# One buffer for the absorbed queries, filled by halves, and queries and turned latents fetched from device memory

## The reference

```python
def xattn(ctx, latents, Wq, Wkv, Wo, ln1, ln2):        # 16 heads of 64
    xn, ln = layernorm(ctx, ln1), layernorm(latents, ln2)
    q = ln @ Wq
    k, v = split(concat([xn, ln], rows) @ Wkv)          # 1024 + 64 rows
    w = softmax(q @ k.T / 8)                            # per batch and head
    return (w @ v) @ Wo
x = x + xattn(ctx, layernorm(x), ...)
x = x + mamba(layernorm(x), ...)                        # 512 inner channels, 16 states
x = x + experts(layernorm(x), ...)                      # 8 experts, given lists
```

## Time and profile before

| | us |
|---|---|
| median of 3 runs | 893.54 (893.11 to 894.03) |
| the profiled execution: time, span | 892.84, 891.1 |
| TensorE busy, share of the span | 788.4, 88% |
| VectorE busy | 531.5, 60% |
| ScalarE busy | 398.1, 45% |
| GpSimd busy | 254.1, 29% |
| mean granted TensorE clock | 0.951 |

### The profile page before, as it was taken

How to read it: one execution, slowest core, us unless ns; L and a number is a source line. 1 busy time by engine, 2 the same in 40 slices (tenths; PEclk the granted TensorE clock), 3 DMA queues, 4 the chain that set the end, 5 groups by cost and what they waited for, 6 DMA issues and landing times.

```text
span 891.1 us, 13590 instructions
## 1 busy us (share of the span) xinstructions
PE 788.4 (88%) x5347; PEld 684.3 (77%) x5347; DVE 531.5 (60%) x992; ACT 398.1 (45%) x952; POOL 254.1 (29%) x173
## 2 busy tenths in 40 slices
PE   5889999999999999999999999997455667598996
PEld 3589999999999999999999999983122323267885
DVE  5365565565565565466556544428899999971112
ACT  3445545543544544454554444434834334403341
POOL 3718018018016105204404400001355555600000
PEclk9999999999999999999999999997759888888998
DMA  9100100100100000010030100000200000070720
GB/s 310 55 1 1 54 1 2 54 2 1 50 5 1 24 32 1 1 54 1 1 125 1 11 1 1 1 1 4 94 0 0 1 0 0 0 270 26 271 95 26
DMA packets 23779, 35.25 MB, mean 40 GB/s; under 512 B 6744, under 2 KB 19616, under 8 KB 22688
## 3 DMA queue, kind: packets, MB, share of 16 engines
q1 hardware_dynamic: 23712, 34.34, 11.7%
HBM read 32.77 MB, written 0.52 MB: 37 GB/s over the span
## 4 chain that ended last, share of the span: by engine, by line
PE 74%; DVE 19%; issue 4%; ACT 1%; DMA 1%; SPq 0%; DVEq 0%; POOL 0%; POOLq 0%
PE psum L1167 21%; PE psum L1201 19%; DVE state L793 11%; PE psum L1184 6%; PE psum L1140 3%; PE psum L1482 3%; PE psum L1472 3%; PE psum L1223 3%; PE psum L1378 2%; PE psum L1123 2%; PE psum L1147 2%; PE psum L1233 2%; PE psum L1214 1%; PE psum L1295 1%; DMA wq_sb<-in_L_xattn_Wq_dram 1%
## 5 line engine op out<-in xcount | busy, mean ns | idle before, releaser
L911 ACT ACTIVATE pt_hi<-psum 128x512 fp32r<-128x512 f32 (+1 forms) x192 | 87.3, 489 | 225.6 <-PE psum L1184 170.4
L1201 PE MATMUL psum<-kvn_hi,pt_hi 128*128 128x256 f32 x512 | 149.6, 292 | 0.0
L1201 PE MATMUL psum<-kvn_hi,pt_lo 128*128 128x256 f32 x512 | 144.1, 281 | 0.0
L1201 PE MATMUL psum<-kvn_lo,pt_hi 128*128 128x256 f32 x512 | 143.9, 281 | 0.0
L643 DVE TENSOR_REDUCE rowmax<-psum 128x1 f32<-128x728 f32 x64 | 58.7, 917 | 110.9 <-PE psum L1167 110.9
L793 DVE TENSOR_TENSOR_SCAN state<-dec,drive 128x2048 f32<-128x2048 f32 x16 | 107.1, 6693 | 0.1
L1201 PEld LDWEIGHTS psum<-kvn_lo,pt_hi 128*128 128x128 f32 x512 | 97.2, 190 | 0.1
L1201 PEld LDWEIGHTS psum<-kvn_hi,pt_hi 128*128 128x128 f32 x512 | 97.1, 190 | 0.1
L1201 PEld LDWEIGHTS psum<-kvn_hi,pt_lo 128*128 128x128 f32 x512 | 97.0, 189 | 0.0
L1167 PE MATMUL psum<-kvt_hi,qk_hi 128*128 128x364 f32 (+1 forms) x384 | 90.9, 345 | 4.5 <-ACT prob L951 2.7
L546 POOL TENSOR_TENSOR drive<-dtx,bmat 128x2048 f32<-128x2048 f32 x15 | 68.4, 4558 | 60.7 <-DVE state L793 60.7
(11 more groups left out here) (214 smaller groups left out, 1452.1 us busy)
## 6 DMA issues: line engine op xcount, KB each, us to landing
w<-in_L_ffn_W_dram SPq DMA_DIRECT2D x16, 1024.0 KB, 7.5
ctx_nat<-in_ctx_dram SPq DMA_DIRECT2D x8, 1024.0 KB, 5.4
wk_nat<-in_L_xattn_Wkv_dram SPq DMA_DIRECT2D x1, 1024.0 KB, 6.3
wq_sb<-in_L_xattn_Wq_dram SPq DMA_DIRECT2D x1, 1024.0 KB, 11.6
wv<-in_L_xattn_Wkv_dram SPq DMA_DIRECT2D x1, 1024.0 KB, 13.7
wo<-in_L_xattn_Wo_dram SPq DMA_DIRECT2D x1, 1024.0 KB, 16.1
lat_cur<-x_lat SPq DMA_DIRECT2D x16, 64.0 KB, 5.0
q_t<-in_L_attn_W_in_dram SPq DMA_DIRECT2D x1, 1024.0 KB, 6.9
```

Source lines behind the costliest of these rows:

```text
L911: act.activation(pt_hi[u][:, t0:t1, :], where[:, 0:(t1 - t0) * P].rearrange("p (t m) -> p t m", m=P), ACT.Copy)\
L1201: pe.matmul(PV, w[u][:, j, :], x_[slot][:, j, :], start=(j == 0 and w is pt_hi and x_ is kvn_hi), stop=False)
```

## The change

`qk_hi` and `qk_lo` have one slot instead of two, 16 KB of each partition less; a filler keeps what follows in place. The halves of a batch's absorbed queries are made at different times: pairs 0 to 3 (jobs 0, 2) for the next batch in steps 3 and 4, when the logits of these pairs are done, and pairs 4 to 7 (jobs 1, 3) in steps 0 and 1 of the batch itself, before its step 4. The order of jobs is `TURNS`, from step 2 of a batch to step 1 of the next: 4, 0, 2, 5, 6, 7, 1, 3. Batch 0 has no job in its steps 0 and 1, and batch 7 has two. Both statistics move into step 0, the first half ahead of the row maximum, and the scaling moves to step 1. `q_t` and `latt` are stored to device memory once; each batch's queries and own rows are loaded from there by SP, and the copies of GpSimd and ScalarE go. The store of `q_t` and the load of the next context are on the same queue, in this order.

```diff
+    TURNS = (4, 0, 2, 5, 6, 7, 1, 3)
+        q_keep = nc.dram_tensor("q_keep", [P, HP, T], F32, kind="Internal").ap()
+        latt_keep = nc.dram_tensor("latt_keep", [P, 2, CK, T], F32, kind="Internal").ap()
-        qk_hi = [sb(att, f"qk_hi{i}", [P, CK, HP, 2, L], F32R) for i in range(2)]
+        qk_hi = sb(att, "qk_hi", [P, CK, HP, 2, L], F32R)
...
         def misc_count(b, m):
-            return MISC * b + m + 1
+            return MISC * b + TURNS.index(m) + 1
+        def misc_of(b, hp, more):
+            if hp < 2:
+                return (b, TURNS[MISC - 2 + hp]) if 0 < b < B else None
+            return (b + 1, TURNS[hp - 2]) if more else None
...
@@ sync
+            def load_own(b):
+                for part, dst in enumerate((kvt_hi, kvt_lo)):
+                    sp.dma_start(dst[b % 2][:, :, S:].bitcast(F32), latt_keep[:, part, :, b * L:(b + 1) * L]).then_inc(ld_own, 16)
+            def load_queries(b):
+                for h in range(2):
+                    rows = slice(h * DH, (h + 1) * DH)
+                    sp.dma_start(q_cur[rows, :, h, :], q_keep[rows, :, b * L:(b + 1) * L]).then_inc(ld_q, 16)
             load_latents(0)
+            sp.wait_ge(s_pevac, 2)
+            sp.dma_start(latt_keep[:, 0], latt_hi[:].bitcast(F32)).then_inc(st_keep, 16)
+            sp.wait_ge(s_plo, 1)
+            sp.dma_start(latt_keep[:, 1], latt_lo[:].bitcast(F32)).then_inc(st_keep, 16)
+            sp.wait_ge(s_pqe, HP)
+            sp.dma_start(q_keep, q_t[:]).then_inc(st_keep, 16)
             for b in range(1, B):
-                sp.wait_ge(s_misc, MISC * b)
+                sp.wait_ge(s_misc, misc_count(b - 1, 7) if b > 1 else MISC)
                 sp.wait_ge(s_klo, b)
                 sp.dma_start(ctx_nat[:], ctx_in[b].rearrange("(p j) c -> p j c", j=SJ))\
                     .then_inc(ld_ctx, 16)
                 sp.wait_ge(s_lcur, 2 * b)
                 load_latents(b)
+                if b == 1:
+                    sp.wait_ge(st_keep, 48)
+                if b >= 2:
+                    sp.wait_ge(s_lg, HP * (b - 1))
+                load_own(b)
+                sp.wait_ge(s_misc, misc_count(b - 1, 3))
+                load_queries(b)
-            sp.wait_ge(s_qcur, 2 * B)
+            sp.wait_ge(s_misc, MISC * B)
@@ gpsimd: def queries(b), two copies into q_cur, and its call go
@@ vector, step
+                if more and hp == 0:
+                    ctx_stats(b + 1, 0)
                 if live:
                     dve.wait_ge(s_lg, count(b, hp))
...
-                if more and hp < MISC - 1:
-                    if hp < 2:
-                        ctx_stats(b + 1, hp)
-                    misc_lo(b + 1, 1 - slot, hp)
-                    if hp == 2:
-                        ctx_scale(b + 1)
+                if more and hp == 0:
+                    ctx_stats(b + 1, 1)
+                if job and hp < MISC - 1:
+                    misc_lo(job[0], job[0] % 2, job[1])
+                if more and hp == 1:
+                    ctx_scale(b + 1)
@@ scalar, step 7
-                    own_rows(b + 1, 1 - slot)
@@ tensor
                     if m == 0:
-                        pe.wait_ge(s_qcur, 2 * b + 2)
+                        if b == 0:
+                            pe.wait_ge(s_qcur, 2)
+                        else:
+                            pe.wait_ge(ld_q, 32 * b)
...
                     if hp == 0:
-                        pe.wait_ge(s_mlo, MISC * (b + 1))
-                        pe.wait_ge(s_own, 2 * (b + 1))
+                        pe.wait_ge(s_mlo, misc_count(b, 7) if b > 0 else MISC)
+                        if b == 0:
+                            pe.wait_ge(s_own, 2)
+                        else:
+                            pe.wait_ge(ld_own, 32 * b)
+                    if hp == HP // 2:
+                        pe.wait_ge(s_mlo, misc_count(b, 3))
```

More of the change, by code:

```diff
@@ L75, in perceiver_kernel @@
         kvt_lo = [sb(att, f"kvt_lo{i}", [P, CK, S + L], F32R) for i in range(2)]
-        qk_hi = [sb(att, f"qk_hi{i}", [P, CK, HP, 2, L], F32R) for i in range(2)]
-        qk_lo = [sb(att, f"qk_lo{i}", [P, CK, HP, 2, L], F32R) for i in range(2)]
+        qk_hi = sb(att, "qk_hi", [P, CK, HP, 2, L], F32R)
+        qk_lo = sb(att, "qk_lo", [P, CK, HP, 2, L], F32R)
         x_lat = sb(att, "x_lat", [P, TT, C])
@@ L83, in perceiver_kernel @@
         latt_lo = sb(att, "latt_lo", [P, CK, T], F32R)
+        sb(att, "rest_of_att", [P, 16 * C])
         q_cur = sb(att, "q_cur", [P, HP, 2, L])
@@ L251, in perceiver_kernel @@
         ld_lat = sem("ld_lat")
+        st_keep, ld_q, ld_own = sem("st_keep"), sem("ld_q"), sem("ld_own")
         ld_mam, ld_idx, ld_comb, ld_b2, ld_out = (sem(n) for n in ("ld_mam", "ld_idx", "ld_comb", "ld_b2", "ld_out"))
@@ L310, in misc_dst @@
                 k, a = m // 2, m % 2
-                return (qk_hi if hi else qk_lo)[slot][:, k, a * HP // 2:(a + 1) * HP // 2]\
+                return (qk_hi if hi else qk_lo)[:, k, a * HP // 2:(a + 1) * HP // 2]\
                     .rearrange("p h a l -> p (h a l)")
@@ L445, in _ @@
             pool.tensor_scalar(lshift[:], lnm[:], -1.0, 0.0, ALU.mult, ALU.add).then_inc(s_psc, 1)
[L447 to L456, removed]
             def latents(b, slot):
@@ L506, in body @@
                 if more:
-                    queries(b + 1)
                     context(b + 1, 1 - slot)
@@ L664, in step @@
                                       ALU.add).then_inc(s_woe, 1)
-                if more and hp == MISC - 1:
-                    misc_lo(b + 1, 1 - slot, hp)
+                job = misc_of(b, hp, more)
+                if job and hp == MISC - 1:
+                    misc_lo(job[0], job[0] % 2, job[1])
                 if p1:
                     tail_lo("C", p1)
-                if more and hp < MISC - 1:
-                    if hp < 2:
-                        ctx_stats(b + 1, hp)
-                    misc_lo(b + 1, 1 - slot, hp)
-                    if hp == 2:
-                        ctx_scale(b + 1)
+                if more and hp == 0:
+                    ctx_stats(b + 1, 1)
+                if job and hp < MISC - 1:
+                    misc_lo(job[0], job[0] % 2, job[1])
+                if more and hp == 1:
+                    ctx_scale(b + 1)
             def body(b, slot, more, pair):
@@ L953, in step @@
                 if more and hp == MISC - 1:
-                    misc_hi(b + 1, 1 - slot, hp)
-                    own_rows(b + 1, 1 - slot)
+                    misc_hi(b + 1, 1 - slot, TURNS[hp - 2])
                 if p1:
@@ L959, in step @@
                     keep_out(p3, pair if hp >= 3 else None)
-                if more and hp < MISC - 1:
-                    misc_hi(b + 1, 1 - slot, hp)
+                job = misc_of(b, hp, more)
+                if job and hp < MISC - 1:
+                    misc_hi(job[0], job[0] % 2, job[1])
             def body(b, slot, more, pair):
@@ L1130, in misc @@
                     pe.wait_ge(s_woe, after)
-                if not (isinstance(b, int) and b == 0):
+                if b > 0:
                     pe.wait_ge(s_mlo, misc_count(b, m) - 1)
@@ L1162, in logits @@
                     for q, x_ in ((qk_hi, kvt_hi), (qk_hi, kvt_lo), (qk_lo, kvt_hi)):
[L1163 removed]
+                        w = q[:, k, hp].rearrange("p a l -> p (a l)")
                         first, final = k == 0 and q is qk_hi and x_ is kvt_hi, k == CK - 1 and q is qk_lo
@@ L1251, in step @@
                     turn_value(p3)
+                job = misc_of(b, hp, more)
                 if slot == 0 and hp == 3 and pair is not None:
-                    out_proj(pair, misc_count(b + 1, hp) - 1)
-                if more and hp == MISC - 1:
-                    misc(b + 1, 1 - slot, hp)
+                    out_proj(pair, misc_count(*job) - 1)
+                if job and hp == MISC - 1:
+                    misc(job[0], job[0] % 2, job[1])
                 if p2:
@@ L1261, in step @@
                     head_out(p3)
-                if more and hp < MISC - 1:
-                    misc(b + 1, 1 - slot, hp, pair + 1 if slot == 0 and hp == 3 and pair is not None else None)
+                if job and hp < MISC - 1:
+                    misc(job[0], job[0] % 2, job[1], pair + 1 if slot == 0 and hp == 3 and pair is not None else None)
             def body(b, slot, more, pair):
```

## The result

The changed kernel takes 909.41 us (median of 4 runs, 907.21 to 911.79) against 893.78 us before (893.11 to 895.04): ratio 1.0174, interval 1.0138 to 1.0209. A second set of 4 runs of the same kernel gave 911.86 against 893.83, ratio 1.0206 (1.0191 to 1.0221). The eight runs are 907.21, 907.49, 910.48, 911.07, 911.33, 911.79, 912.64 and 913.62. Forecast were 907.4 in a range of 899 to 913. The profiled execution took 911.79 with a span of 910.1, 19.0 us more than before.

What follows compares the result with a forecast made beforehand. TensorE was taken to bound the attention part, so only its added waits or work cost time: 8.5 + 3.4 + 0.2 + 1.8 = 13.9 us on the median 893.54 gives 907.4, range 904 to 910 (899 to 913 with A and most of B).

Steps and rivals of the forecast that it cites:

- part 1: Step 2, batches 0 to 6: context transposes wait for GpSimd's add because scaling moves only one step earlier; 8.5 us slower.
- part 2: Batch 0: statistics ahead of the first row maximum wait for the context, plus query store; 3.4 us; later batches free.
- clock: Batch 0: one stretch of TensorE's lower clock after the longer wait, now wholly behind the restart; 0.2 us.
- part 3: Batch 7, steps 0 and 1: two query jobs gained at 0.89 us each, 1.8 us; batch 0's two lost save nothing.
- part 4: GpSimd's and ScalarE's copies become stores and loads on SP's queue; gain 0, cost 0, nothing waits for the loads.
- its own signs: Seven step-2 waits, context wait until 43 to 45 us, second logits near 49.4; wrong if start over 9 us late.
- A: Rival: the step-2 wait does not appear, something else holds TensorE or scaling comes earlier; 898.9 us, chance 0.09.
- B: Rival: the query store is slow and the start pays its upper bound, context 6.2 us later; 912.6 us, chance 0.10.
- D: Rival: ScalarE and VectorE's exchange sets step length, so removed copies and moved statistics save time; 893.4 or 891.6 us, chance 0.04.
- E: Rival: the step-2 wait is absent and the start hidden too, only part 3 is left; 895.3 us, chance 0.05.
- C: Rival: each of seven new waits brings a stretch of TensorE's lower clock, 12 us more; 919 us, chance 0.04.
- the fast bound of the prediction: Query store at 434 GB/s, gone by 38.3 before the context's bytes move, cost 0; the slow bound was 175 GB/s.

Runs made afterwards that it cites:

- e1: The changed kernel with the prologue's eight jobs counted 1 to 8 again in ScalarE's and VectorE's waits: 908.61 us against 893.96, ratio 1.0169.
- e3: The changed kernel with VectorE scaling the next context ahead of the job's low half in step 1: 904.53 us against 893.96, ratio 1.0122.
- e4: e1 with the store of the queries issued behind the load of context 1 and the latents: 909.07 us against 908.61 for e1.
- e5: The kernel before, with only the prologue waits of ScalarE and VectorE asking for counts in the new job order: 899.52 us against 893.96, ratio 1.0064.
- e6: Edits of e1, e2 and e3, and batch 0's jobs 1 and 3 moved from prologue to its steps 0 and 1: 893.99 us against 893.83, ratio 1.0001.
- e2: e1 with batch 0's first half of the statistics behind the first row maximum again: 904.55 us against 893.96, ratio 1.0125.

## Why the prediction was right, and where it was not

The time lay in the range, 2.0 us above the forecast by the first set and 4.5 by the second. That it lies so near is in part luck: a cost that was not forecast stands where a forecast one is hidden. The mechanism is borne out by e1, the kernel that the prediction had in mind: from its first logits to the end of the attention its steps fall behind by 13.8 us against the kernel before (14.2 from span to span, 14.7 by the medians), where 13.9 was forecast. Its parts one by one, with e1 where the changed kernel covers a part:

| step | forecast, us | measured, us |
|---|---|---|
| part 1, batches 1 to 6 | 7.74 | 7.69 (1.17 for odd, 1.38 for even ones) |
| part 1, batch 0 | 0.75 | 0.85 in e1 (steps 2 to 5) |
| part 2, batch 0, and clock | 3.4 + 0.2 | 3.48 in e1 (steps 0 and 1) |
| part 2, batches 1 to 7 | 0 | 0.00 |
| part 3 | 1.8 | 1.80 |
| part 4 | 0 | 0, no wait for the loads |
| prologue | 0 | 5.74, of which 4.9 by the counts |

**Part 1** was right in mechanism and size. GpSimd's add ends at 137.55 + 2.35 = 139.90, and the transpose that TensorE could have begun at 138.90 starts at 140.05. All engines of the changed kernel, batch 1, to be set against the earlier trace rows:

```profile
132.32 2.67 DVE L623 TENSOR_SCALAR ctx_nat<-ctx_nat,crstd,cshift 128x256 f32<-128x256 f32 x8
...
135.07 2.40 POOL L510 TENSOR_TENSOR ctx_nat<-ctx_nat,ln1wb 128x1024 f32<-128x1024 f32 x1 [8.55 <-DVE ctx_nat L623]
...
137.55 2.35 POOL L512 TENSOR_TENSOR ctx_nat<-ctx_nat,ln1wb 128x1024 f32<-128x1024 f32 x1
...
140.05 0.63 PE L1175 MATMUL psum<-ident,ctx_nat 128*128 128x128 f32 x4 [1.15 <-POOL ctx_nat L512]
```

The distance from scaling to transpose, read one step later in the trace before, held to 0.02 us a batch. One thing the forecast passed over cancels: the transposes are 0.5 us shorter than the query product whose place they take in step 2, and step 4 gets that product and 0.5 us more (8.27 to 8.77). e3 shows that the order on VectorE is the cause.

**Part 2** holds for the kernel that the prediction had in mind. In e1 the context landed at 44.9 (forecast 44.4) and the second logits started at 49.80 (49.4). The forecast gave 1.0 us of this to the store; the landing took 6.8 us in e1 and 5.6 to 6.2 in the other profiles with the store ahead, against 5.2 before, so the size is about right, but its reason stays open (see e4). In the changed kernel itself this wait did not appear: VectorE was busy with the late low parts until 44.64, and then found the context landed. The wait that was forecast is hidden behind the one that was not.

**The step that failed** is the prologue. The prediction costs `misc_count` only inside the batches, and takes the first logits as unmoved. The edit of one helper changed the sense of another caller's argument. What hangs on it could be read before: there the last query product ended, and only 1.7 us of waiting for its low part stood ahead of the logits, because the copies of all earlier groups had run beside the products. What the runs showed in place of an unmoved start are 5.74 us, 4.9 of them by the counts (e5, e1). The late counts put 4.9 us on the start and hide most of the 3.5 us of part 2. With it comes the clock: 0.72 granted over the 31 us from 39 to 70 is (1 - 0.72) x 2 x 31 = 17 us at the lower level (1.2 GHz), against (1 - 0.94) x 2 x 31 = 4 before. Beside e3 this costs 26.35 - 23.50 = 2.8 us in steps 0 to 2, where the forecast had 0.2 for the clock. Batch 1 begins 9.1 us late, where parts 1 and 2 gave 0.75 + 3.4 + 0.2 = 4.35.

By its own signs the prediction was thus half met in the changed kernel. The waits of step 2 and the two long steps of batch 7 are there. The wait for the context in batch 0 is not, the second logits start at 53.16 and not at 49.4, and the start, read at batch 1, is late by 9.1 and 8.7 us in the two profiles, about the 9 us that it named as a sign of being wrong. One sum is also off: the parts' own bounds give 904 to 911, not 904 to 910.

**Part 4**: the page's DMA issues (count, KB each, median us to landing), to be set against the earlier trace rows:

```profile
q_keep<-q_t SPq DMA_DIRECT2D x1, 2048.0 KB, 8.5
q_cur<-q_keep SPq DMA_DIRECT2D x14, 128.0 KB, 2.9
...
lat_cur<-x_lat SPq DMA_DIRECT2D x16, 64.0 KB, 5.1
...
kvt_hi<-latt_keep SPq DMA_DIRECT2D x7, 64.0 KB, 4.3
```

A load of queries, twice the size of a latent load, landed in 2.9 us, and 17 us were there; no engine waits for `q_cur` or the own rows from batch 1 on. Of the rivals, **A** was excluded by the first line of the waits, **B** by the landing of the context (5.6 to 6.8 us with the store ahead against 5.2 before, not 6.2 later; that the second set's 911.9 lies near B's 912.6 is luck), **D** by steps 6, 7 and 0, which are as long without the copies as with them, to 0.01 us. **E** falls with A. **C** did not happen: the six waits of 1.1 to 1.2 us lie in this stretch, and the granted clock stays full (changed kernel, columns as above):

```profile
105.00:600.00 495.00, 487.30 (x3905) 471.15 (x3903) 274.91 (x704) 235.32 (x614) 116.44 (x73) 1.00 0.09 24
```

The swing of the clock that the Trainium skill ("TensorE: Matmul & The Clock Gate", A second HAM failure mode) tells of was thus not met with idle moments of this length in every eighth step. The store of 2 MB landed 8.5 us after its issue (6.3 in e6), but its bytes moved at 378 GB/s over the 5.5 us from 33.0 to 38.5 (rows at e4), near the fast bound of the prediction (434) and far from the slow one (175). By the limit of about 358 GB/s in the Trainium skill ("DMA: Bandwidth & Descriptors", Specifications) the bytes alone would take 5.9 us, as an estimate. The trace has them through in 5.5, and the measurement decides.

## What to carry to other kernels

When an order is renumbered, look at every caller of the helper that maps it, above all at those that pass a position instead of a name; a wait that asks for too late a count changes nothing but the time. One that asks for too early a count breaks the order of the data: here the last four copies asked for 1, 4, 5 and 6 where they need 5 to 8, and only the fourth copy's wait for count 8 ahead of them covers that. To price a moved step, look for the same pair of operations at the new distance elsewhere in the old trace and read when its consumer would have been ready. A first iteration that waits has room for work: two jobs moved there from the prologue cost nothing and took 1.2 us from the way to the first logits. And one landing does not prove a term: read the same quantity in the profiles of all kernels that share it. Between e1 and e4 lie 1.1 us, but so do they between e1 and e2, which have the same order on the queue.

## What was not expected of the hardware

Waits of the same length did not bring the same clock. In the changed kernel waits of 6.60, 3.54 and 0.75 us stand ahead of the first three logits, and the granted clock from 39 to 70 us is 0.72 in both profiles; in e3 they are 6.60, 3.55 and 0.75, and it is 0.89. A wait of 2.7 us ahead of the second logits is followed by 0.56 in the kernel before and by 1.00 in e6. The first three logits of step 1 took 1.27 us in the changed kernel (53.16) and 0.77 in e3 (53.45). What decides it is open. A start with waits therefore has a cost that one profile does not settle: here 2.8 us.

And the start is not steady: the projection of the queries, the same 32 matmuls, took 15.42 to 16.93 us in the ten profiles, and began between 15.89 and 16.99. That is as large as some terms above. A single profile settles the length of a wait, not the last microseconds of the time.
